# Where VectorE's first memory update stands in a period of linear attention, and how its background work is shared out over the period

## The reference, cut to what matters

```
x  = x + attn(cond(x, f))            # 4 batches x 512 tokens x 512 channels
out = x + ffn(cond2(x, f))

cond:  forward and backward decaying sums over the tokens of exp(k)*v and exp(k),
       y = sigmoid(r) * num / max(den, 1e-8) * const
attn:  q, k, v = y @ Wq, y @ Wk, y @ Wv            # 16 heads of 128
       for each of the 4 segments of 128 tokens in turn, per batch and head,
       from mem = 0, z = 1/128:
         scores  = q k^T / sqrt(128), causal;  att_dot = softmax(scores) @ v
         att_mem = sigma(q) @ mem / (sigma(q) @ z)       # sigma = elu + 1
         delta   = v - sigma(k) @ mem / (sigma(k) @ z)
         mem    += sigma(k)^T @ delta;  z += sum(sigma(k))
         att     = beta * att_mem + (1 - beta) * att_dot
       attn = att @ Wo
ffn:   (silu(y W1) * (y W3)) -> Walsh-Hadamard over 2048 -> W2
```

## Time and profile before

| what | us |
|---|---|
| three runs | 1851.23, 1853.14, 1853.37 (median 1853.14) |
| the profiled execution | 1851.23 |
| its span, first to last instruction | 1849.4 |
| TensorE busy in it | 1626.1 |
| VectorE busy in it | 1175.9 |
| ScalarE, GpSimd busy | 654.6, 531.1 |
| period 14 (no background steps) | 26.3 |
| period 18 (a usual one) | 27.8 |
| period 16 (a burst) | 50.5 |
| TensorE's granted clock, mean | 0.956 of full speed |

### The profile page before, as it was taken

One profiled execution on the slowest core, in us unless ns is written; L12 is line 12 of the kernel. 1 busy time (PEld: TensorE's weight loads), 2 busy tenths in 40 slices (PEclk: granted clock), 3 DMA queues, 4 the chain that ended last, 5 costly groups with the idle time before them and its releaser, 6 DMA issues.

```text
span 1849.4 us, 26600 instructions
## 1 busy us (share of the span) xinstructions
PE 1626.1 (88%) x9696; PEld 1435.5 (78%) x9696; DVE 1175.9 (64%) x2672; ACT 654.6 (35%) x1491; POOL 531.1 (29%) x418
## 2 busy tenths in 40 slices
PE   1489978998998999998897888877889999999999
PEld 0378867897897898897896778766768888888887
DVE  8699969997996698997885655444323333333333
ACT  2355625535534534534534342453211111111111
POOL 6466575122121132121110100031044333333311
PEclk9689998999999999999999889898999999999999
DMA  3285485575364365454346326343711001000002
GB/s 102 57 298 188 165 302 187 194 247 187 110 240 171 140 222 209 140 217 155 135 188 254 120 97 257 131 135 136 258 61 35 23 16 31 23 24 23 12 0 91
DMA packets 101697, 258.08 MB, mean 140 GB/s; under 512 B 10768, under 2 KB 27584, under 8 KB 100928
## 3 DMA queue, kind: packets, MB, share of 16 engines
q1 hardware_dynamic: 82992, 229.12, 34.4%
q10 hardware_dynamic: 18576, 27.27, 5.0%
HBM read 206.00 MB, written 50.35 MB: 139 GB/s over the span
## 4 chain that ended last, share of the span: by engine, by line
PE 62%; DVE 20%; DMA 6%; issue 6%; ACT 3%; SPq 1%; POOL 1%; ACTq 0%; DVEq 0%; POOLq 0%
PE psG L373 11%; PE psG L375 10%; PE psG L374 10%; PE psX L373 3%; PE psX L374 3%; PE psX L375 3%; DMA HA<-in_w 2%; PE psZ L508 2%; PE psX L527 2%; PE psX L480 2%; DVE S L820 2%; PE psY L373 2%; PE psY L375 2%; PE psY L374 2%; DVE DBK L760 2%
## 5 line engine op out<-in xcount | busy, mean ns | idle before, releaser
L373 PE MATMUL psG<-yh,wh 128*128 128x512 f32 x632 | 261.7, 414 | 22.4 <-DVE xb L895 12.2
L375 PE MATMUL psG<-yh,wl 128*128 128x512 f32 x632 | 251.3, 398 | 0.0
L374 PE MATMUL psG<-yl,wh 128*128 128x512 f32 x632 | 251.3, 398 | 0.0
L1474 POOL TENSOR_TENSOR vs<-v,omb 128x512 f32<-128x512 f32 x64 | 91.2, 1445 | 410.0 <-PE psX L527 406.6
L373 PE MATMUL psG<-wh,yh 128*128 128x256 f32 x512 | 156.8, 306 | 49.4 <-POOL yl L1446 49.4
L1482 POOL TENSOR_TENSOR hl<-sg,hh 128x512 fp32r<-128x512 f32 x64 | 82.5, 1290 | 343.5 <-ACT hh L1262 343.5
L1411 POOL TENSOR_TENSOR wl<-stage,wh 128x512 fp32r<-128x512 f32 x112 | 159.1, 1431 | 66.0 <-ACT wh L1066 60.8
L373 PEld LDWEIGHTS psG<-yh,wh 128*128 128x128 f32 x632 | 122.1, 193 | 45.9 <-issue 17.6
L373 PE MATMUL psG<-ah,wh 128*128 128x256 f32 x512 | 147.3, 288 | 4.2 <-DVE al L874 2.4
L374 PE MATMUL psG<-wl,yh 128*128 128x256 f32 x512 | 148.9, 291 | 0.0
L375 PE MATMUL psG<-wh,yl 128*128 128x256 f32 x512 | 148.7, 290 | 0.0
(11 more groups left out here) (185 smaller groups left out, 4219.9 us busy)
## 6 DMA issues: line engine op xcount, KB each, us to landing
wh<-high_o SPq DMA_DIRECT2D x56, 512.0 KB, 5.1
wl<-low_o SPq DMA_DIRECT2D x56, 512.0 KB, 6.4
wh<-high_v SPq DMA_DIRECT2D x24, 512.0 KB, 4.8
wl<-low_v SPq DMA_DIRECT2D x24, 512.0 KB, 6.3
wh<-high_k SPq DMA_DIRECT2D x24, 512.0 KB, 4.7
wl<-low_k SPq DMA_DIRECT2D x24, 512.0 KB, 5.9
wh<-high_q SPq DMA_DIRECT2D x24, 512.0 KB, 4.7
wl<-low_q SPq DMA_DIRECT2D x24, 512.0 KB, 6.1
```

The costliest lines, as they stand in the source:

```text
L373: e.matmul(out, lh, rh, start=first, stop=False, skip_group_check=check)
L374: e.matmul(out, lh, rl, start=False, stop=False, skip_group_check=check)
L375: return e.matmul(out, ll, rh, start=False, stop=last, skip_group_check=check)
L1474: e.tensor_tensor(vs[:, :, j, :], v[n % 2][:, :, j, 0:P], omb[:, 128 * j:128 * j + 128].rearrange("p (a d) -> p a d", a=1).to_broadcast([P ...
```

## The change

In `vector`, the second sigma of q and the first memory update now come right after the first sigma; the low part of the attention and the background steps of slot 0 come behind them. The rooms of the slots are changed as well: slot 0 gets none, slots 2, 4, 6 and 7 of a usual period get more and slot 3 less. In a burst, slot 1 gets 1500 instead of 1400, slot 2 3300 instead of 2200. The sums stay 12,000 and 30,600. The rooms hold for all engines.

```
--- before.py
+++ after.py
@@ -63,8 +63,8 @@
                                   for name, cost in HADAMARD if (name, i) != ("mult", 0)] + [("mult", 7, 300)]
 STEPS += [(name, b, cost) for b in range(2) for name, cost in MODULATE]
 NSLOT = 8
-ROOM = (1300, 1500, 1700, 2100, 1500, 1100, 1300, 1500)
-BURST_ROOM = (1200, 1400, 2200, 5500, 3600, 4800, 2900, 9000)
+ROOM = (0, 1500, 2200, 1500, 2500, 1100, 1500, 1700)
+BURST_ROOM = (0, 1500, 3300, 5500, 3600, 4800, 2900, 9000)
 
 
 def is_burst(n):
@@ -972,12 +972,12 @@
                 maxima(n, 0)
                 maxima(n, 1)
                 sigma(n, "q", 0)
-                behind(n, 0)
+                sigma(n, "q", 1)
+                memory(n, 0)
                 if n > 0:
                     low_att(n - 1)
-                sigma(n, "q", 1)
+                behind(n, 0)
                 behind(n, 1)
-                memory(n, 0)
                 if not more:
                     gate(0, 0, "1", G[0])
                 behind(n, 2)
```

## The result

| | before | changed |
|---|---|---|
| median of 9 runs each, us | 1851.23 | 1858.48 |
| lowest and highest, us | 1844.92, 1854.44 | 1853.77, 1864.58 |
| the profiled execution, us | 1851.23 | 1861.83 |
| its span, us | 1849.4 | 1860.0 |
| VectorE busy in it, us | 1175.9 | 1164.9 |

The ratio is 1.0041, with a 95% interval of 1.0023 to 1.0059: slower by 0.4%, outside the forecast's 0.2% of "same", inside its wide range of 1847 to 1863 us and half a us beyond its own range of 1850 to 1858. The three runs before had a median of 1853.14 us, the nine here 1851.23.

The account below looks back on a forecast made before the run. VectorE and TensorE were both taken as close to the bound in the periods. 17 us of new waits against 15 us of gains summed to +1.5 us on the 1853.14 median: 1854.6 us, range 1850 to 1858, wide range 1847 to 1863.

Parts of the forecast that it names:

- rival 2: VectorE bounds also where gains were counted; early wins are spent by period 4: 1862 us; slower, chance 0.32.
- usual periods: Eleven usual periods with background: VectorE idles before the first update, delaying the third update and recall 3: +9.3 us.
- periods after bursts: Periods 5, 9, 17, 21: VectorE idles before a late first update, delaying recall 3 in most: together +1.7 us.
- bursts 4 to 24: Six bursts: VectorE idles before the first update, so the second update and recall 2 come later: +5.5 us.
- period 13: The 2.66 us wait before recall 1 goes, and most of the slow clock stretch behind it: -4.1 us.
- periods 0 and 1: Period 0's 4.01 us wait before recall 1 goes, with slow clock: -5.2 us; period 1 wins 2.7.
- periods 25 to 30: Hadamard periods: VectorE waits for the load of HA wherever the level stands: sum -0.2 us.
- period 31 and after: z_low begins 5 us sooner and the second z_load follows, shortening the 9.94 us wait at the scores: -2.8 us.
- wrong if L508 doesn't wait more: Sign against the forecast: TensorE's waits for mem at L508, recall 3, should rise from 12.5 to 25 us or more.
- Rival 3: A queue other than VectorE's sets the periods' pace: 1851 to 1856 us; chance 0.43 together with the forecast.
- I cost them at nothing: ScalarE's and GpSimd's shares of the moved steps cost nothing, since both have idle time in every period.
- theory A: From the follow-up runs: the order costs VectorE's idle time before the first update, being short of time further on.

Follow-up runs that it names:

- e3: The changed kernel with ScalarE's copy of v's second half ahead of slot 2's background steps in bursts: 1856.21 us.
- e4: The changed kernel with only the low part of the attention put back between the two sigmas: 1832.31 us.
- e9: The kernel before, old rooms, with the low part behind the first update and slot 0's background steps still between the sigmas: 1853.47 us.
- e10: The changed kernel plus one VectorE sum per period, result unread, ahead of the second sigma of q: 1859.67 us.
- e11: The kernel before plus one VectorE sum per period, result unread, ahead of the second sigma of q: 1889.79 us.
- e1: The changed order of VectorE's steps with the rooms of the kernel before: 1877.37 us, ratio 1.0144 to before.
- e2: The kernel before with the new rooms only, order unchanged: 1833.54 us, ratio 0.9899 to before.

## Why the prediction was right, and where it was not

The forecast said 1854.6 us and "about no change, 17 us of new waits against 15 us of gains"; it was 1858.5, on the slower side, between the forecast and rival 2. I gave "same" 0.43 and "slower" 0.32, and it is slower, clear of noise. The difference was forecast as +1.5 us and is +7.2; the time is 3.9 us off and not 5.7 because the median that I started from was 1.9 us above that of the nine runs. The sum's terms against the two profiled executions, in us:

| term | forecast | measured |
|---|---|---|
| usual periods | +9.3 | +1.8 |
| periods after bursts | +1.7 | +1.8 |
| bursts 4 to 24 | +5.5 | +19.4 |
| period 13 | -4.1 | -3.3 |
| periods 0 and 1 | -7.9 | +1.0 |
| periods 25 to 30 | -0.2 | -8.7 |
| period 31 and after | -2.8 | -1.4 |
| sum | +1.5 | +10.6 |

So the total was near by errors that cancel, not term by term: that part is luck. A term of one execution is no sharper than some 5 us in the last row: e3, whose edit touches the bursts alone, has 601.5 us from period 31 on, the change 606.8.

- **VectorE idles 1.4 us before the first update**: right, in place, size and number of periods, and e4, e9, e10 and e11 show that this is the order's cost. The step that failed was where it is paid. I had it at recall 3 (L508 from 12.5 to 25 us or more; it came to 14.0). It is paid at update 1, which waits for `t` 9.3 us in periods 0 to 24 and didn't before, and in the bursts. By my own list ("wrong if L508 doesn't wait more") this part of the mechanism was wrong, though VectorE's idle time was not.
- **Usual periods, mis-sized at +9.3.** "The same arithmetic with each period's own durations" was the step. Durations don't move along with a step: in period 18 L742 and L756 each came out 1.0 us shorter. Over the eleven usual periods, what VectorE's instructions take beyond their usual time beside GpSimd fell from 32.9 to 26.6 us (the last section has the count), against 7.5 us that the term was off. VectorE's busy time in periods 2 to 24 fell by 6.2 us in the changed kernel; e1, with the old rooms, has over half of that (702.4 against 706.0 in its row of that stretch). Rival 3 named the wrong queue, ScalarE's, where GpSimd's instructions beside VectorE's mattered; in the bursts ScalarE's was the right one.
- **Bursts, mis-sized at +5.5.** The step that failed is "I cost them at nothing" of the other queues. The named risk, an exponential of ScalarE that waits for VectorE ahead of copy_v, came true with 3.14 us in burst 8 and 3.86 in burst 12 (1.77 there before), against "up to 1.5". The waits belong to the order: with the rooms alone (e2) the row for v is 3.3 us and bursts 4 to 24 are 1.7 us longer than before, all told. To that comes the clock, for which I had "taken no new one": 0.57 over 8 us in burst 8. Of the clock only a part comes each time: burst 24 has 0.94 in the profiles of the change, e3 and e10 alike, and 1.00 in those of before and e2, but burst 8 has 0.94, 0.97 and 1.00 in the first three. In bursts 16 and 20 the forecast's own mechanism holds: new waits of 1.92 and 1.09 us for `mem` before the second recall, and 2.4 and 1.4 us more, where I had 1.6 and 1.0.
- **Period 13** was right: no wait before recall 1, and the stretch at the lower clock right behind it is gone too. Recall 1 stands at 599.09 there, and the stretch behind it reads:

```profile
600.00:604.00 4.00, 3.83 (x28) 3.29 (x26) 3.97 (x9) 1.17 (x3) 0.49 (x1) 1.00 0.00 0
```

- **Periods 0 and 1, mis-sized at -7.9.** The wait of 4.01 us is gone, but recall 1 was not what the period waits for. Two new waits take its place:

```profile
105.95 0.82 PE L499 MATMUL psZ<-delta,kn 128*128 128x129 f32 x4 [2.58 <-DVE t L851]
...
114.61 1.65 PE L527 MATMUL psX<-vs,pT 128*128 128x128 f32 x6 [4.08 <-ACT pT L1212]
```

The second one waits for ScalarE, which stands in front of a weight load in both kernels. Its rows in the changed kernel:

```profile
111.85 1.22 ACT L1066 ACTIVATE wh<-stage 128x512 fp32r<-128x512 f32 x2 [13.16 <-DMA stage<-in_wv]
...
113.97 1.08 ACT L1212 ACTIVATE pT<-psY 128x512 f32<-128x512 f32 x2
```

The copy of pT stood at 114.19 before the change and stands at 113.97 now. A load that comes at 111.8 in both kernels was the bound behind the bound, and I had not looked at it. The trace of before would have shown this.

- **Periods 25 to 30** gained 8.7 us, which I had not seen coming. Of that 3.4 us is TensorE's busy time at a clock of 0.94 instead of 0.91. The wait of 6.5 us before the second recall of period 25 is gone altogether. Before the change VectorE's load-bound step L782 stood ahead of that recall's update and waited 7.00 us for its data:

```profile
1015.45 0.69 DVE L782 TENSOR_TENSOR HB<-HA 128x512 f32<-128x512 f32 x1 [7.00 <-DMA HA<-in_w]
...
1018.33 0.80 PE L507 MATMUL psZ<-mem,sk 128*128 128x129 f32 x2 [6.51 <-DVE mem L834]
```

  In the changed kernel it stands behind that update, and 2.97 us of the wait come back at update 2. Period 25 is 38.9 us long instead of 44.2, and that takes both parts of the change: with the order alone it is 43.5 (e1), with the rooms alone 44.2 (e2). The rooms alone bring 4.9 us of the 8.7 (e2: 248.3 us for the six periods against 253.2), all of it in periods 26 to 29; the order alone nothing (e1: 252.9). Burst 24, just in front, got 4.7 us longer, so some of the gain is only passed on.
- **Period 31.** The wait at the scores is 4.53 + 0.87 = 5.4 us instead of 9.94: 4.5 us less, more than the 2.4 I had. But 2.3 us of it come back as TensorE's busy time behind it (577.3 against 575.1 us in the last stretch), and 1.4 us in two later waits of TensorE, one for VectorE's `xb` and one that the profile puts down to nobody, which last 7.3 us each instead of 6.6.

What stays open: how much of the bursts' 19.4 us is the clock's luck in one execution. e10, with the same order and rooms, has 14.9 us there, and e3, without the wait for v, 12.3. Open too is why 31 us of new idle time cost 26 us in e1, and not more or less: theory A gives the place and the sign, and the differences that I wrote down by it were too small in e1, e2, e4 and e11.

## What to carry to other kernels

An early release of a waiting engine pays only if the releasing engine has nothing better to do in the meantime: look for the moment at which its *input* can be there, put exactly as much other work in front as fits, and leave the rest behind. Here that was 1.4 us of room, and one 1.2 us step in it was worth 20 us or more over 31 periods. When a change has two parts, run each alone: here +26 and -18 us hid behind +7. And follow a removed wait one station further, to the load or queue that ends the next one.

## What the runs showed of the hardware

- **VectorE's instructions last up to 1.1 us longer beside GpSimd's.** In the profile before, 137 instructions of VectorE last over 0.15 us longer than the median of their line and shape away from GpSimd, 113.5 us in all. Every one of them overlaps an instruction of GpSimd. After the change it is 127 and 100.9 us, again all beside GpSimd. One case: L742 began at 755.37 inside GpSimd's EKV product (754.82 to 756.59) and ended at 757.13, 0.54 us behind it; alone it takes 0.74 us. In the changed kernel the same product ran from 772.87 to 774.16, and now L738, begun at 772.99, ended at 774.71, 0.55 behind it, with 0.69 as its usual time. It goes the other way as well: the first of the two products began 0.06 us behind L738 (754.76, 0.69 us) and took 1.77 us, the second 1.29.

```profile
772.87 1.29 POOL L1417 TENSOR_TENSOR EKV<-EK,kx 128x512 f32<-128x512 f32 x1 [11.51 <-ACT EK L1071]
```

  The Trainium skill (SBUF — State Buffer, "SBUF: two separate sides") says that the two engines share a port pair which whoever starts first holds for its whole instruction, when VectorE's has two inputs in SBUF or runs in a mode that uses two ports. By that the second one waits and then runs; the rows agree in this, though what comes after GpSimd's end is 0.14 to 0.20 us less than a whole instruction. L742 and L738 have two inputs; L756 has one, and no run here shows its mode. L742 has 30 instances and a mean that went from 1048 to 1204 ns with the change, while VectorE's busy time as a whole fell by 11 us: a reordering deals these collisions out anew.
- **The same wait is not always followed by the same clock.** In burst 8 of the changed kernel TensorE waits 3.14 us for v, and the 8 us from 396, in which the wait ends, have 0.57. In e10, the same order and rooms, it waits 3.13 us at the same place, and the clock stays up behind it:

```profile
397.44 0.36 PE L374 MATMUL psG<-ah,wh 128*128 128x256 f32 x1 [3.13 <-ACT v L1194]
```

```profile
398.00:406.00 8.00, 8.00 (x72) 8.00 (x71) 7.86 (x13) 2.23 (x4) 2.17 (x2) 1.00 0.59 179
```

  The burst is 55.5 us long in the one and 52.8 in the other. One profiled execution can thus differ from the next by some 3 us in one burst, against 7.2 us for the whole change.
